# Ranking edges by source with accumulating VectorE operations, and degree terms carried by the first walk

## The reference

```python
# layer 0 (GraphSAGE, mean of the neighbours)
neigh_sum = segment_sum(feat[src], dst)
deg = segment_sum(ones, dst)
h = concat([feat, neigh_sum / maximum(deg, 1.0)[:, None]]) @ W_neigh + b_neigh
x = layernorm(x + h)
# layer 1 (GCN2, two propagations; sums run by src over x[dst])
deg = segment_sum(ones, col)              # col: dst, and a loop at every node: 1 + the degree above
norm = deg ** -0.5 [row] * deg ** -0.5 [col]
h = segment_sum(norm[:, None] * x[col], row)
xp = 0.9 * h + 0.1 * x
```

## Time and profile before

| | |
|---|---|
| median of the runs | 5191.07 us |
| the profiled execution | 5192.05 us, span 5190.1 |
| busy in the span | TensorE 3396.3 us, VectorE 3401.2, ScalarE 2337.2, GpSimd 3490.4 |
| first walk (e0), with the sort | from about 72 us to the last matmul at 487.4 |
| first node stage | from 488 us to about 893 |
| second walk (e1a) | first gather 915.9, last matmul 1174.5 |

### The profile page before, as it was taken

The page is one execution under the profiler, slowest core; times in us unless marked ns, Lnnn a source line. Parts: engine busy times, 40 slices in busy tenths (PEclk is TensorE's granted clock), DMA queues, the critical chain, the costliest instruction groups (busy, mean ns, idle before and its releaser), DMA issues. The chain is left out here.

```text
span 5190.1 us, 95540 instructions
## 1 busy us (share of the span) xinstructions
PE 3396.3 (65%) x21145; PEld 2503.1 (48%) x21146; DVE 3401.2 (66%) x12799; ACT 2337.2 (45%) x6751; POOL 3490.4 (67%) x4335
## 2 busy tenths in 40 slices
PE   0566776777778699969949999941001999431566
PEld 0465665676756344422236667631000777321566
DVE  6996666544468577668848888851441888642776
ACT  0343665676757444423338888820000444100466
POOL 3760886777735577726758888867575555673999
PEclk9988999999989899979979999965555999755788
DMA  2332665888899742101124444443112999352576
GB/s 76 103 119 97 203 206 170 247 258 243 262 238 282 246 138 53 53 20 35 38 73 142 144 140 139 145 125 96 33 41 88 295 293 292 119 148 55 168 225 198
DMA packets 593106, 784.81 MB, mean 151 GB/s; under 512 B 138946, under 2 KB 362870, under 8 KB 592330
## 3 DMA queue, kind: packets, MB, share of 16 engines
q1 hardware_dynamic: 431734, 533.20, 33.2%
q0 software_dynamic: 62848, 112.43, 8.9%
q10 hardware_dynamic: 98328, 137.22, 7.2%
HBM read 470.23 MB, written 317.95 MB: 152 GB/s over the span
## 5 line engine op out<-in xcount | busy, mean ns | idle before, releaser
L2902 POOL TENSOR_SCALAR n_hot<-node_of,d_krel 128x256 f32<-128x256 f32 x396 | 381.1, 976 | 65.2 <-ACTq L2958 65.2
L1350 ACT ACTIVATE n_r<-n_r,n_shift,n_rstd 128x128 f32<-128x128 f32 x784 | 321.6, 480 | 79.4 <-POOL n_shift L1341 73.4
L2930 PE MATMUL n_bank<-h_rows,n_hot 128*128 x1584 | 239.2, 319 | 145.4 <-POOL n_hot L2902 144.4
L998 POOL DMA_INDIRECT x_rows<-x,d_other_i x196 | 237.1, 1210 | 118.8 <-POOLq L102 59.4
L684 POOL DMA_INDIRECT agg<-e_msg,e_put_i x196 | 194.8, 994 | 165.4 <-DVEq L713 114.1
L2930 PEld LDWEIGHTS n_bank<-h_rows,n_hot 128*128 128x128 f32 x1584 | 226.8, 230 | 158.5 <-issue 158.5
L1350 ACT ACTIVATE n_o<-n_y_ps,n_shift,n_rstd 128x128 f32<-128x128 f32 x784 | 292.6, 453 | 16.9 <-POOL n_shift L1637 16.8
L1057 PE MATMUL e_bank<-x_rows,e_hot 128*128 x1584 | 225.3, 310 | 91.6 <-DVE e_hot L1013 77.1
L1057 PEld LDWEIGHTS e_bank<-x_rows,e_hot 128*128 128x128 f32 x1584 | 216.8, 221 | 100.4 <-issue 100.4
L615 POOL DMA_INDIRECT agg_dst<-e_rows,e_put_i x196 | 195.2, 996 | 102.0 <-issue 59.4
L2523 POOL TENSOR_TENSOR n_u<-n_u 128x512 f32<-128x512 f32 x98 | 124.5, 1271 | 206.0 <-DVE n_u L2470 206.0
(11 more groups left out here) (522 smaller groups left out, 11625.1 us busy)
## 6 DMA issues: line engine op xcount, KB each, us to landing
n_ag<-agg_dst SPq DMA_DIRECT2D x196, 264.0 KB, 2.9
n_hs<-h SPq DMA_DIRECT2D x196, 264.0 KB
n_xs<-x SPq DMA_DIRECT2D x196, 256.0 KB, 4.2
agg_dst<-e_ev SPq DMA_DIRECT2D x196, 132.0 KB
y<-n_o ACTq DMA_DIRECT2D x98, 264.0 KB, 2.8
e1a_fed<-y SPq DMA_DIRECT2D x196, 132.0 KB
m<-e1a_ev SPq DMA_DIRECT2D x196, 132.0 KB
e1b_fed<-m SPq DMA_DIRECT2D x196, 132.0 KB
```

The source lines that it names most:

```text
L998: pool.indirect_dma_start(out=rows[:, c, 0:fetched], out_offset=None, in_=table, in_offset=bass.IndirectOffsetOnAxis(ap=e.other_i[:, c:c + ...
L1350: ins = act.activation(out[:, g, 0:D], r[:, g, :], ACT.Identity, bias=shift[:, g:g + 1], scale=rstd[:, g:g + 1])
L2902: ins = pool.tensor_scalar(hot[:, i // STEPB % HOTS, i % STEPB, :], keep.node_of[:, :], e.krel[:, i:i + 1], None, ALU.is_equal)
L2930: ins = pe.matmul(bank[:, bass.ds(to + h * 256, SUMMED)], hot[:, s, k, h * P:(h + 1) * P], flat_rows[:, bass.ds(row, SUMMED)], start=False ...
```

## The change

The sort: a digit's count is one `tensor_scalar` over the 196 digits of a partition (equal to d, summed into one column of `hist`), 196 of them; a place is one `scalar_tensor_tensor` over a row that holds the digits 0 to 195 and then the digits of the partition's edges (equal to the edge's digit, times a row that holds the bases and then ones, summed into one column of `place`), 196 of them, 196 to 391 columns wide. Each waits only for the fourth before it, whose output buffer it takes. Places come four to a batch, behind batches 2 to 50.

The degrees: the four words beside the features start in the walk from (1, 11/9, 0, 0) and grow by (1, 2/9, 1, 0) an edge. So the sums arrive with degree + 1, its 2/9 plus 1, and the degree. GpSimd's `degree` goes; `factor` is one product of two words of `ag`, at lag 2; VectorE's maximum with 1 writes both degrees. SP loads a slot of `ag` only when `factor` has read it.

```diff
-FEW = 7
+FEW, FOUND = 4, 4
 PLACES_FROM = 2
...
-        self.beside, self.key_i = ph.sb("beside", [P, digits + J], F16), ph.sb("key_i", [P, J], I32)
-        self.same, self.earlier = ph.sb("same", [P, FEW, digits + J], F16), ph.sb("earlier", [P, FEW, FEW], F16)
...
+        self.beside, self.dig = ph.sb("beside", [P, digits + J], BF16), ph.sb("dig", [P, J])
+        self.adds, self.found = ph.sb("adds", [P, digits + J]), ph.sb("found", [P, FOUND, digits + J], BF16)
...
+        self.base = self.adds[:, 0:digits]
...
         dve.memset(self.one_row[:, :], 1.0)
-        dve.tensor_tensor(self.earlier[:, :, :], keep.iota_h[:, 0:FEW].unsqueeze(1).broadcast_to([P, FEW, FEW]),
-                          keep.iota_h[:, 0:FEW].unsqueeze(2).broadcast_to([P, FEW, FEW]), ALU.is_lt)
+        dve.memset(self.adds[:, digits:digits + J], 1.0)
...
-        self.link(dve.tensor_copy(self.dig, self.key_i[:, :]))
-
-    def count_digits(self, dve, d):
-
-        same = self.same
-        self.link(dve.tensor_tensor(same[:, :, 0:J], self.dig.unsqueeze(1).broadcast_to([P, FEW, J]),
-                                    self.beside[:, d:d + FEW].unsqueeze(2).broadcast_to([P, FEW, J]), ALU.is_equal))
-        self.link(dve.tensor_reduce(self.hist[:, d:d + FEW], same[:, :, 0:J], AX.X, ALU.add))
-        if d + FEW == HIGH:
-            dve.tensor_copy(self.hist_h[:, :], self.hist[:, :]).then_inc(self.hist_ready, 1)
+        dve.tensor_copy(self.dig[:, :], self.key_i[:, :])
+        self.link(dve.tensor_copy(self.beside[:, digits:digits + J], self.key_i[:, :]))
+
+    def count_digits(self, dve):
+
+        for d in range(HIGH):
+            if d >= FOUND:
+                dve.wait_ge(self.counted, d - FOUND + 1)
+            dve.tensor_scalar(self.found[:, d % FOUND, 0:J], self.beside[:, HIGH:HIGH + J], float(d), None, ALU.is_equal, ALU.add,
+                              accum_out=self.hist[:, d:d + 1]).then_inc(self.counted, 1)
+        dve.wait_ge(self.counted, HIGH)
+        dve.tensor_copy(self.hist_h[:, :], self.hist[:, :]).then_inc(self.hist_ready, 1)
...
     def find_places(self, dve, c):
 
-        digits, same, wide = HIGH, self.same, HIGH + c + FEW
-        self.link(dve.tensor_tensor(same[:, :, 0:wide], self.beside[:, 0:wide].unsqueeze(1).broadcast_to([P, FEW, wide]),
-                                    self.dig[:, c:c + FEW].unsqueeze(2).broadcast_to([P, FEW, wide]), ALU.is_equal))
-        dve.tensor_tensor(self.base_of[:, :, :], same[:, :, 0:digits], self.base[:, :].unsqueeze(1).broadcast_to([P, FEW, digits]), ALU.mult)
-        self.link(dve.tensor_tensor(same[:, :, wide - FEW:wide], same[:, :, wide - FEW:wide], self.earlier[:, :, :], ALU.mult))
-        dve.tensor_reduce(self.place[:, c:c + FEW], self.base_of[:, :, :], AX.X, ALU.add)
-        self.link(dve.tensor_reduce(self.before_it[:, c:c + FEW], same[:, :, digits:wide], AX.X, ALU.add))
+        for k in range(c, c + FEW):
+            if k >= FOUND:
+                dve.wait_ge(self.summed, k - FOUND + 1)
+            dve.scalar_tensor_tensor(self.found[:, k % FOUND, 0:HIGH + k], self.beside[:, 0:HIGH + k], self.dig[:, k:k + 1],
+                                     self.adds[:, 0:HIGH + k], ALU.is_equal, ALU.mult, accum_out=self.place[:, k:k + 1])                .then_inc(self.summed, 1)
...
-                    if b >= PLACES_FROM and (b - PLACES_FROM) % 2 == 0 and (b - PLACES_FROM) // 2 < J // FEW:
-                        by_source.find_places(dve, (b - PLACES_FROM) // 2 * FEW)
+                    if 0 <= b - PLACES_FROM < J // FEW:
+                        by_source.find_places(dve, (b - PLACES_FROM) * FEW)
...
+    DEGREES = (1.0, 1.0), (11.0 / 9.0, 2.0 / 9.0), (0.0, 1.0), (0.0, 0.0)
...
-        dve.memset(self.zeros[:, :, :], 0.0).then_inc(self.zeroed, 1)
-        dve.memset(rows[:, :, D:ROW], 1.0)
+        dve.memset(self.zeros[:, :, 0:D], 0.0).then_inc(self.zeroed, 1)
+        for i, (first, each) in enumerate(self.DEGREES):
+            dve.memset(self.zeros[:, :, D + i:D + i + 1], first).then_inc(self.zeroed, 1)
+            dve.memset(rows[:, :, D + i:D + i + 1], each)
...
                     sp.wait_ge(turned[s], used)
+                    sp.wait_ge(added[s], used)
                     sp.dma_start(ag[:, s], block_rows(agg, turn, s)).then_inc(ag_in[s], 16)
...
-                def degree(turn, s):
-
-                    st = Steps(pool, pool_step, turn * SLOT + s, 1)
                     done(pool, ag_in, turn, s, 16)
-                    free(pool, sums_ready, turn, s)
-                    free(pool, meaned, turn, s)
-                    free(pool, added, turn, s)
-                    pool.tensor_tensor(q[:, s, 0, :], ag[:, s, :, D], keep.ones[:, 0:GB], ALU.add).then_inc(counted[s], 1)
...
-                    pool.tensor_tensor(o[:, s, :, D + 1], part[:, s, :], q[:, s, 0, :], ALU.mult).then_inc(added[s], 1)
+                    pool.tensor_tensor(o[:, s, :, D + 1], ag[:, s, :, D + 1], ag[:, s, :, D], ALU.mult).then_inc(added[s], 1)
...
-                pipeline(pool, (0, degree), (4, factor), (0, sort), written_out=True)
+                pipeline(pool, (2, factor), (0, sort), written_out=True)
...
-                    st(dve.tensor_scalar(q[:, s, 1, :], ag[:, s, :, D], 1.0, None, ALU.max))
+                    free(dve, sums_ready, turn, s)
+                    free(dve, inverted, turn, s)
+                    st(dve.tensor_scalar(q[:, s], ag[:, s, :, D:ROW:2].rearrange("p g i -> p i g"), 1.0, None, ALU.max))
                     st.wait()
-                    done(dve, counted, turn, s)
-                    free(dve, inverted, turn, s)
                     st(dve.reciprocal(rq[:, s], q[:, s]))
```

More of the change, by code:

```diff
@@ L874, in tile_rows @@
     return a.rearrange("(b p h) d -> b p h d", p=P, h=2)[bass.ds(turn * TILE_TURN + k, 1)].squeeze(0)
-FEW = 7
+FEW, FOUND = 4, 4
 PLACES_FROM = 2
-assert HIGH == J and J % FEW == 0 and PLACES_FROM + 2 * (J // FEW) <= BATCHES
+assert HIGH <= LOW and J % FEW == 0 and PLACES_FROM + J // FEW <= BATCHES
 class BySource:
@@ L904, in memory @@
             ph.sem(n) for n in ("hist_ready", "sums_done", "sums_read", "placed"))
-        self.dig = self.beside[:, digits:digits + J]
+        self.counted, self.summed = ph.sem("counted"), ph.sem("summed")
     def load(self, sp):
@@ L1022, in _ @@
                 by_source.find_digits(dve)
-                for d in range(0, HIGH, FEW):
-                    by_source.count_digits(dve, d)
+                by_source.count_digits(dve)
                 by_source.find_base(dve)
@@ L1397, in node_sage @@
 def node_sage(nc, keep, x_turned, agg, w, bias, y1, by_source):
-    with Phase(nc, "n0", freed="turned added stored y_ready x1_ready sums_ready meaned inverted") as ph:
+    with Phase(nc, "n0", freed="turned added stored y_ready x1_ready inverted sums_ready") as ph:
         wa, wb, b, b_rest = ph.sb("wa", [P, D]), ph.sb("wb", [P, D]), ph.sb("b", [1, D]), ph.sb("b_rest", [1, D])
@@ L1406, in node_sage @@
         ag = ph.sb("ag", [P, SLOT, GB, ROW])
-        shift, q, part = ph.sb("shift", [P, SLOT, GB]), ph.sb("q", [P, SLOT, 2, GB]), ph.sb("part", [P, SLOT, GB])
-        rq, ninths = ph.sb("rq", [P, SLOT, 2, GB]), ph.sb("ninths", [P, GB])
-        counted, mixed, meaned, inverted = (slot_sems(ph, n) for n in ("counted", "mixed", "meaned", "inverted"))
-        mean_steps, pool_step = ph.sem("mean_steps"), ph.sem("pool_step")
+        shift, q, rq = ph.sb("shift", [P, SLOT, GB]), ph.sb("q", [P, SLOT, 2, GB]), ph.sb("rq", [P, SLOT, 2, GB])
+        meaned, inverted, mean_steps = slot_sems(ph, "meaned"), slot_sems(ph, "inverted"), ph.sem("mean_steps")
         o = ph.sb("o", [P, SLOT, GB, ROW])
@@ L1448, in _, with factor @@
             def _(pool):
-                pool.wait_ge(cleared, 2)
-                def degree(turn, s):
-                    st = Steps(pool, pool_step, turn * SLOT + s, 1)
+                pool.wait_ge(cleared, 1)
+                def factor(turn, s):
                     done(pool, ag_in, turn, s, 16)
-                    free(pool, sums_ready, turn, s)
-                    free(pool, meaned, turn, s)
-                    free(pool, added, turn, s)
-                    pool.tensor_tensor(q[:, s, 0, :], ag[:, s, :, D], keep.ones[:, 0:GB], ALU.add).then_inc(counted[s], 1)
-                    done(pool, counted, turn, s)
-                    st(pool.tensor_tensor(part[:, s, :], q[:, s, 0, :], ninths[:, :], ALU.mult))
-                    st.wait()
-                    pool.tensor_tensor(part[:, s, :], part[:, s, :], keep.ones[:, 0:GB], ALU.add).then_inc(mixed[s], 1)
-                def factor(turn, s):
-                    done(pool, mixed, turn, s)
                     free(pool, stored, turn, s, 16)
-                    pool.tensor_tensor(o[:, s, :, D + 1], part[:, s, :], q[:, s, 0, :], ALU.mult).then_inc(added[s], 1)
+                    pool.tensor_tensor(o[:, s, :, D + 1], ag[:, s, :, D + 1], ag[:, s, :, D], ALU.mult).then_inc(added[s], 1)
                 def sort(turn, s):
```

18 lines of the change are left out of this document (8 added, 10 removed).

## The result

The changed kernel takes 5011.41 us (median of four runs, 5006.86 to 5015.89) against 5189.0 for the kernel before: a ratio of 0.966, with a 95% interval of 0.9643 to 0.9677. The forecast was 5026 (5025 at the median's level), in 4978 to 5098. The profiled execution took 5015.89 us, span 5014.2.

What follows compares the result with a forecast made beforehand. VectorE was taken to bound the first walk and GpSimd the first node stage. From the profiled 5192 us, 109 for the walk and 57 for the node stage came off: 5026 us (5025 at the median's level), range 4978 to 5098.

Steps and rivals of the forecast that it cites:

- Count: VectorE's digit count ahead of the first walk's matmuls: 196 accumulating instructions at 0.29 us, 57 us instead of 90.7.
- The nearest row: Profile row of L1936's product and sum, one every 0.21 us at 128 columns, from which 0.29 us a count was estimated.
- the rival in which accumulating costs its whole length: In count and places, each instruction and read ends before the next begins: total 5074 to 5106 us; chance 0.17.
- Places: VectorE's ranking of edges in the first walk: 196 instructions at 0.475 us on average, 93 us in all.
- The walk: First walk, to TensorE's last matmul: 238 us long, ending at 378, 109 us earlier than before.
- the pace of TensorE: TensorE's own time per batch in the first walk: 3.39 us, from the last eight batches before the change.
- 3.9 at the last batch: VectorE's predicted time for the last walk batch with places, rising from 3.25 us at the first.
- Gathers: GpSimd's gathers in the first walk: pass between VectorE's short instructions, about 0.95 us each, done by 320.
- The rival that starves them: In the first walk, VectorE's unbroken trains keep GpSimd from writing gather descriptors: slower, 5248 us; chance 0.04.
- Node stage: First node stage: block period falls from 3.88 to 3.3 us, ScalarE next behind GpSimd, saving 57 us over 98 blocks.
- ScalarE's own block: ScalarE's period per block in the first node stage: 3.88 less its 0.67 wait for VectorE, 3.21 us.
- SP's new wait: First node stage: loads of a block's sums wait until GpSimd has read the tile's last use; costed at nothing.

Runs made afterwards that it cites:

- e4: The kernel after, but each accumulating instruction of the sort waits for the one directly before it, not four back: 5038.41 us.
- e5: The kernel after with all 196 places ranked behind the last batch of one-hots, none between batches: 5092.92 us.
- e7: The kernel after with two more 128x4 copies on ScalarE in each block of the first node stage: 5023.8 us.
- e15: The kernel after with 100 digits counted before the first walk, and the first node stage's stores issued by SyncE instead of ScalarE: 4992.86 us.
- e9: The kernel after with the row of digits and the accumulating instructions' outputs in F32 instead of BF16: 5015.72 us.

## Why the prediction was right, and where it was not

*Count.* Taken as 0.29 us each and 57 in all; measured 0.277 and 54.3. Its end was to come at 133.5, the first matmul at 140.3; they came at 130.6 and 137.2. The nearest row (the product and sum of the earlier trace rows) was the right one, and e4 shows the reason given, the wait four instructions back, to be the cause: without it 0.40 us, on the way to the 0.45 to 0.53 of the rival in which accumulating costs its whole length.

*Places.* Taken as 0.475 us in the mean; by e5, where they run by themselves, 0.34 us at 196 columns and 0.54 at 380, 87 us in all (373.73 to 461.00 in its order of time) instead of 93. Right.

*The walk.* Its end was to be 378 and was 381.6, but the working behind it was wrong. The step that failed is the pace of TensorE, 3.39 us a batch, read from the last eight batches of before; in e5, with VectorE out of the way, it is 3.72. The sample was not the steady pace. Its first two batches ran in one train with the batch ahead of them, with no gap between. Behind a wait of 3.70 us that train's first matmuls start 0.22 us apart and not 0.11 (granted clock 0.62 from 455.5 to 460), and TensorE's loads and checks for the next batch were through by 459.2, ahead of its first matmul at 460.28:

```profile
455.85 9.99 PE L1057 MATMUL e_bank<-x_rows,e_hot 128*128 x72 [3.70 <-DVE e_hot L1013]
```

And the gathers were over; near the walk's end TensorE's gaps between batches are 0.47 us (after, from 342.93) and not 0.65. Every third batch pays 0.4 us more for the turn of the loop. I put 40 batches on VectorE at 3.76 us and 26 on TensorE at 3.39, 238 us; TensorE's side needs 245 with no places beside it (e5). That the sum fitted is luck: VectorE's batches with places (3.2 us from 141.87 to 145.08, 3.8 from 234.00 to 237.79, 4.07 from 320.38 to 324.45 in its order) came out around TensorE's true pace, and where they are longer, the lead of up to three batches covers them. (The prediction's 3.9 at the last batch is a slip: 1.79 and four places of 0.59 make 4.1. Its sum uses 3.76 and is not touched.) So the 70 us within the walk are the step from VectorE's old pace to TensorE's, not to VectorE's new one.

*Gathers.* Predicted to pass between short instructions, 0.95 us each and out by 320; they did, 0.947 us in the median, none above 1.25, the last start at 322.3. The rival that starves them is refuted: at 1.27 us from start to start they went faster than before, beside a VectorE that was busy 54.9 of 55 us.

*Node stage.* Taken as 3.3 us a block and 57 us; measured 3.17 and 74. GpSimd fell away as the bound as predicted. The term that was mis-sized is ScalarE's own block: 3.21 was the old period less one wait of 0.67, with 0.1 for hand-overs on top; a third of ScalarE's blocks in after take 2.9 to 3.0 us. The one wait that I subtracted was not ScalarE's only idle time in the block. And that ScalarE is the next bound held only in part: 20 us of copies on it cost 8.9 (e7), and taking its store away gained 1.3 (e15).

*SP's new wait.* Costed at nothing, rightly. SyncE's waits in the node stage of after (420 to 700 us; us in total, times, longest) have one row, and it names TensorE, not GpSimd:

```profile
SPq L1443 <- PE n_y_ps L1490: 176.9, 87, 2.4
```

The two errors lie on opposite sides, +4 us in the walk and -17 in the node stage; the median came out 14 us below the 5025 forecast for it.

## What to carry to other kernels

When a stage's bound is taken away, work out the next engine's pace over whole turns of its loop, not over the last few iterations, and test it by taking the first engine's extra work away altogether: VectorE was busy 39.9 of 40 us, and with 87 us of places taken off it the walk ended where it did. The engine that a view of waits names behind a gap came last; whether it was waited for is seen in what the waiting engine did in the gap. Accumulating instructions overlap with the read of their accumulator only when the next one does not wait for it, so let a buffer's wait look several instructions back. And compare stage by stage by marks in the trace: the common rest of this program differed by up to 15 us between these executions, and six of the twelve experiments changed the total by less than that.

## What was not expected of the hardware

- A third copy per tile on ScalarE cost no time: 0.90 us a tile with two instructions and a wait of 0.22 us for TensorE, or with three and no wait. The walk was 4.7 us shorter (239.7 against 244.4), which no run explains.
- A turn of TensorE's loop of three batches costs 0.4 us; with 33 batches to a turn, the one turn showed a gap of 4.98 us, of which the branch at its end took 4.32 in the trace (0.21 in the median of all such branches).
- TensorE's register loads from a table took 0.33 us at least (L1044, after). One that starts behind a batch's last weight load makes, with the checks behind it, the 0.65 us between batches.
- An accumulating comparison of 196 columns takes 0.277 us from start to start with BF16 or F32 in and out (e9), and a place 1.06 ns more for each further column (0.34 at 196, 0.51 at 356).
- TensorE's granted clock over the walk was 1.00 of full speed, the level of 2.4 GHz, against 0.88 before (175 to 485 us), when it waited for one-hots again and again; its matmuls took 281 ns in the mean instead of 310.
